# Two fused transformer layers: the next pair's norm moved out of the opening's units, VectorE's first round written out, the first MLP chunk computed by sequence

## The reference

```python
h = (x - mu) * jax.lax.rsqrt(var + LN_EPS)
h = h * (1.0 + scale[:, None, :]) + shift[:, None, :]
q = (h @ Wq.T) ...; c_kv = h @ Wkd.T; k = (c_kv @ Wku.T) ...; v = (c_kv @ Wvu.T) ...
out = softmax(mask(q k / sqrt(d))) @ v;  x = x + out @ Wo.T        # layer 0
...
h = ada_rms(x, time_emb, ln1_w, ln1_tw);  attention as above, 8 heads  # layer 1
x = res + ctx @ Wo.T
h = ada_rms(x, time_emb, ln2_w, ln2_tw)
mlp = jax.nn.silu(h @ Wg.T) * (h @ Wu.T) @ Wd.T
return res + mlp
```

## Time and profile before

| | us |
|---|---|
| median of 3 runs (lowest, highest) | 1760.81 (1760.7, 1761.95) |
| the profiled execution | 1759.8 |
| its span, first to last instruction | 1758.0 |
| PE busy, share of the span | 1703.3, 97% |
| DVE busy | 1148.6, 65% |
| ACT busy | 943.9, 54% |
| POOL busy | 407.1, 23% |

### The profile page before, as it was taken

One profiled execution on the slowest core, in us unless ns is written; L12 is line 12 of the kernel. 1 busy time (PEld: TensorE's weight loads), 2 busy tenths in 40 slices (PEclk: granted clock), 3 DMA queues, 4 the chain that ended last, 5 costly groups with the idle time before them and its releaser, 6 DMA issues.

```text
span 1758.0 us, 37788 instructions
## 1 busy us (share of the span) xinstructions
PE 1703.3 (97%) x12440; PEld 929.4 (53%) x12440; DVE 1148.6 (65%) x2850; ACT 943.9 (54%) x2769; POOL 407.1 (23%) x569
## 2 busy tenths in 40 slices
PE   6777999999999999999999999999999999999999
PEld 3445545555555545565455555555455554556444
DVE  6757675766768568675677767686576866767320
ACT  3936475453855447364674547555484645735320
POOL 3648694111211011011110212110120111102120
PEclk9797999999999999999999999999999999999999
DMA  8966599454866359472793548753584717935310
GB/s 257 166 189 115 159 249 218 92 83 115 194 142 114 76 138 194 96 129 67 175 190 79 91 118 174 163 104 85 123 199 97 139 59 168 198 79 97 115 60 25
DMA packets 527228, 234.24 MB, mean 133 GB/s; under 512 B 476336, under 2 KB 493744, under 8 KB 527024
## 3 DMA queue, kind: packets, MB, share of 16 engines
q1 hardware_dynamic: 511472, 175.09, 49.9%
q10 hardware_dynamic: 15552, 56.63, 10.3%
HBM read 90.09 MB, written 16.78 MB: 61 GB/s over the span
## 4 chain that ended last, share of the span: by engine, by line
PE 82%; DMA 3%; DVE 1%; issue 1%; ACT 0%; SPq 0%; DVEq 0%; ACTq 0%
PE up L1522 9%; PE up L1523 9%; PE up L1524 9%; PE gate L1522 9%; PE gate L1523 9%; PE gate L1524 9%; PE y L1524 4%; PE y L1523 4%; PE y L1522 4%; PE bank L1522 4%; PE bank L1524 4%; PE bank L1523 4%; PE bank L1549 2%; DMA prob_t<-prob 2%; PE bank L1593 2%; PE bank L1557 1%
## 5 line engine op out<-in xcount | busy, mean ns | idle before, releaser
L907 ACT ACTIVATE bank<-bank,low 128x128 f32<-128x128 f32 (+2 forms) x768 | 302.5, 395 | 66.6 <-DVE low L1164 36.9
L731 POOL TENSOR_TENSOR inner_t<-inner,inner_t 128x512 f16<-128x512 f32 x128 | 150.9, 1179 | 637.4 <-ACT inner_t L1103 637.3
L1171 DVE TENSOR_TENSOR prob<-bank,prob 128x512 f16<-128x512 f32 (+1 forms) x304 | 192.7, 634 | 42.9 <-ACT prob L916 41.6
L916 ACT ACTIVATE prob<-bank 128x512 f16<-128x512 f32 (+1 forms) x304 | 169.5, 558 | 59.1 <-DMA prob_t<-prob 41.1
L1477 DVE SCALAR_TENSOR_TENSOR silu<-silu,gate 128x512 f32<-128x512 f32 x128 | 87.9, 687 | 167.7 <-ACT silu L1097 166.6
L1522 PE MATMUL gate<-mlp,ring 128*128 128x512 f16 x512 | 193.9, 379 | 2.1 <-DVE silu L1477 1.2
L1522 PE MATMUL up<-mlp,ring 128*128 128x512 f16 x512 | 193.8, 379 | 0.6 <-DVE inner L1487 0.6
L1524 PE MATMUL gate<-mlp,ring 128*128 128x512 f16 x512 | 194.0, 379 | 0.0
L1523 PE MATMUL gate<-mlp,ring 128*128 128x512 f16 x512 | 193.9, 379 | 0.0
L1524 PE MATMUL up<-mlp,ring 128*128 128x512 f16 x512 | 193.9, 379 | 0.0
L1523 PE MATMUL up<-mlp,ring 128*128 128x512 f16 x512 | 193.9, 379 | 0.0
(11 more groups left out here) (183 smaller groups left out, 4050.5 us busy)
## 6 DMA issues: line engine op xcount, KB each, us to landing
ring<-wgu_dram ACTq DMA_DIRECT2D x108, 512.0 KB, 3.9
x_in<-x_dram SPq DMA_DIRECT2D x18, 512.0 KB, 3.8
x_res<-x_mid SPq DMA_DIRECT2D x16, 512.0 KB, 3.0
wgu_dram<-ring SPq DMA_DIRECT2D x16, 512.0 KB, 3.5
out_dram<-x_res SPq DMA_DIRECT2D x32, 256.0 KB, 2.3
inner_t<-wd_t_dram SPq DMA_DIRECT2D x4, 1024.0 KB, 9.5
ring<-wg_t_dram SPq DMA_DIRECT2D x16, 256.0 KB, 4.2
ring<-wu_t_dram SPq DMA_DIRECT2D x16, 256.0 KB, 4.6
```

Of the source, the lines that this page charges most:

```text
L731: pool.tensor_tensor(inner_t[:, 1, f, :], inner[:], inner_t[:, 0, f, :], ALU.subtract).then_inc(inner_low, 1)
L907: ins = act.activation(bank_[:, at:at + wid], bank_[:, at:at + wid], ACT.Exp, bias=low[:, j % BANKS, k:k + 1], scale=-1.0, accum_out=total)
L916: act.activation(terms(prob_place(n, g)[:, 0, :], layer, j), terms(work_bank[USE[f"unit{layer}", j] % BANKS][:], layer, j), ACT.Copy).then ...
L1171: dve.tensor_tensor(terms(place[:, 1, :], layer, j), terms(work_bank[USE[name] % BANKS][:], layer, j), terms(place[:, 0, :], layer, j), AL ...
```

## The change

Four edits:

- DVE's first round is written out ahead of its loop with the constant pair, so that `FIRST_PARTS` holds on DVE too.
- The first round's `FIRST_PARTS` begin with 4, 0 and not with 0, 4: the four parts of chunk 0 stand ahead of `fill0.0`.
- These four parts become `opening_part`: gate of sequence 0, up of sequence 0, gate of sequence 1, up of sequence 1, each 12 matmuls with 256 columns. Each gate part waits only for the low halves of its own sequence.
- In the opening, the next pair's `ln_stats` go to `out1b`, ahead of each `add`, its `ln_apply` behind `fill4`, and POOL's `ln_root` to `fill4.0`, ahead of `root`.

```diff
-FIRST_PARTS = [0, 4, 3, 1, 2, 1, 0, 0, 2, 1, 4, 0, 2, 2, 4, 0, 0, 4, 3, 1, 2, 3, 1, 2, 1, 1, 2, 1,
+FIRST_PARTS = [4, 0, 3, 1, 2, 1, 0, 0, 2, 1, 4, 0, 2, 2, 4, 0, 0, 4, 3, 1, 2, 3, 1, 2, 1, 1, 2, 1,
...
@@ GpSimd, layers @@
+                    if m is None and step == "fill4.0":
+                        for s in BOTH:
+                            ln_root((n[0], n[1] + 1), s)
                     if step in ("fill2.0", "fill4.0"):
                         for s in BOTH:
                             root(n, ("fill2.0", "fill4.0").index(step), s)
-                    if step in LN_STATS:
+                    if m is not None and step in LN_STATS:
...
@@ VectorE, units @@
-                    if step in LN_STATS:
+                    if m is not None and step in LN_STATS:
                         ln_stats((n[0], n[1] + 1), LN_STATS[step])
-                    elif step in LN_APPLY:
+                    elif m is not None and step in LN_APPLY:
...
@@ VectorE, finish @@
                 for s in BOTH:
+                    if m is None and layer == 1:
+                        ln_stats((n[0], n[1] + 1), s)
                     add(n, layer, s, 1)
...
@@ VectorE, layer1, behind fill4 @@
+                if m is None:
+                    for s in BOTH:
+                        ln_apply((n[0], n[1] + 1), s)
...
@@ VectorE, rounds @@
-            with dve.Fori(0, NP - 1) as i:
-                layer0((i, 1), (i, 0))
-                layer1((i, 1), (i, 0))
+            layer0((None, 1), (None, 0))
+            layer1((None, 1), (None, 0))
+            with dve.Fori(0, NP - 2) as i:
+                layer0((i, 2), (i, 1))
+                layer1((i, 2), (i, 1))
...
@@ TensorE @@
+            def opening_part(part):
+                s, kind = part // 2, part % 2
+                n = (None, 0)
+                bank_, full = ((gbank, g_full), (ubank, u_full))[kind]
+                tokens = slice(s * TOK, (s + 1) * TOK)
+                if kind == 0:
+                    need(pe, low_made, count(n, LOW_USES, LOW_USE["fill4", s, 1] + 1))
+                if s == 0:
+                    if kind == 0:
+                        pe.wait_ge(chunk_split, 1)
+                    need(pe, d_read, count(n, DT, DT - 1 + kind))
+                for c in range(CH):
+                    w = tuple(ring[:, 0, kind, half, c, :] for half in range(2))
+                    ins = product(bank_[:, tokens], w, cut(mlp_t, slice(None), c, tokens),
+                                  c == 0, c == CH - 1)
+                if s == 1:
+                    ins.then_inc(full, 1)
```

More of the change, by code:

```diff
@@ L1738, in layer1 @@
                 between(m, "end")
+            def opening_part(part):
[15 more added lines that the diff above has]
+                    ins.then_inc(full, 1)
             def mlp_part(n, part):
+                if n[0] is None and n[1] == 0 and part < 4:
+                    opening_part(part)
+                    return
                 if part < 4 * FCH:
```

## The result

| | before | after |
|---|---|---|
| median of 20 runs each, in turn on the same chip, us | 1761.84 | 1764.55 |
| lowest and highest, us | 1759.13, 1764.86 | 1759.86, 1768.37 |
| the profiled execution, us | 1759.8 | 1765.89 |
| its span, us | 1758.0 | 1764.1 |

The ratio of the medians is 1.0016, with a 95% interval of 1.0010 to 1.0022: the change is 2.7 us slower. That is less than the 0.2% taken as the bound, but the interval lies wholly above 1, the time lies outside the range, and the sign is the opposite of the forecast's.

What follows compares the result with a forecast made beforehand. PE was taken to bound the steady rounds, so only the opening and first round could give time: -3.6 - 0.2 + 0.5 - 0.1 = -3.4, 1757.4 us for the median; range 1755.0 to 1760.2.

Steps and rivals of the forecast that it cites:

- The units, -3.6: Opening's layer 1 units: without the norm on DVE, ACT's last copy comes 3.6 us earlier; bounds -1.0 and -4.0.
- The norm's new place: Opening's handover: statistics hide in DVE's waits for PE; POOL's root queue makes the first scaling 1.0 us later.
- The second scaling: RMS norm at the last fill: POOL makes its root by 176.75, as before (176.76), so it does not come later.
- Chunk 0 by sequence, and `lat`: Up to the second fill, -0.2 us; then +0.5 for later conversions, with 0.4 of PE's wait ahead of `lat`.
- The rival of the clock: Output projections after the units: if the clock stays low through both, +10.4 us, 1767.8 us; chance 0.04.
- If the clock rose earlier, it would not grow: Opening's units: an earlier clock rise would not raise the 3.6 us gain, since ACT holds the pace.
- The first round, -0.1 with bounds of -1.7 and +1.5: DVE following `FIRST_PARTS`: -1.1 at chunk 4's gate step, +0.4 around unit 20, +0.6 given back.
- The gate step ahead of unit 20: First round: chunk 15's gate step moves ahead of unit 20's low half; PE's scores wait 1.05 us more.
- the 0.6 for what an earlier PE gives back by waiting for others: First round, 223 to 300 us: full DMA engines make an earlier PE wait, returning 0.6 of the 1.1 us gained.
- the first round takes it back: Rival: earlier PE only waits longer at full DMA engines (+0.8), conversions cost 1.5; sum -1.5, 1759.3 us; chance 0.15.
- the sign of error: PE's idle time from 223 to 300 us growing by more than 1 would show the forecast wrong.
- The steady rounds are PE's, every PE instruction there stays, and nothing in this change can shorten them: From 420 us PE is busy throughout, so only the opening and first round can give time.

Runs made afterwards that it cites:

- best1: Changed kernel with POOL's roots reordered, chunk 15's gate step back, 104 unread matmuls in the opening's last eight layer 1 units, 30 VectorE memsets: 1.0005 to before.
- after_gate15: Changed kernel with chunk 15's gate step put back at unit 21, behind unit 20's low half, in VectorE's first round: ratio to before 1.0008.
- after_gates: Changed kernel with the gate steps of chunks 4 and 15 both put back in VectorE's first round: ratio to before 1.0008.

## Why the prediction was wrong

- **The units, -3.6: right.** -3.74, by ACT's pace; of the nine other kernels with the norm's move eight gained 3.5 to 3.8 there, and best1, with unread matmuls in the units, 2.8.
- **The norm's new place: right.** The statistics hid behind the projections, and the roots cost the 1.0 us of POOL's queue at the last fill that was written down. The second scaling, which was to stay in place, came 0.6 us late as well. Swapping the roots gives 1.0 us back at `kv`.
- **Chunk 0 by sequence, and `lat`: nearly right.** The 256-column matmuls lie 0.109 us apart at full clock, and the wait ahead of `lat` is 0.40 as forecast. From the fill to `kv` 0.7 us were to be gained (the 1.0 that the fill was late, 0.2, less 0.5), 0.15 were: the first gate matmul came 3.56 us behind the fill, not 3.3, and chunk 0 took 5.41 us, not 5.2, as the fills and the first three gate matmuls ran at the lower clock.
- **The rival of the clock: the right mechanism, the wrong point and size.** It asked whether the clock would have risen by the projections and gave it 0.04, "PE is the fuller now, not the emptier". The clock rose earlier, which made PE the emptier by time, and in the profiled execution it fell again just ahead of the projections. That cost 1.5 us, not 10.4. "If the clock rose earlier, it would not grow" was the place to ask what an early rise does later.
- **The first round, -0.1 with bounds of -1.7 and +1.5: failed.** It was +3.15. PE's place, followed from `kv` matmul by matmul in both traces, gives the parts: 1.3 us gained at chunk 5's gate, as described; 0.6 lost at the inner step behind it and 1.3 at POOL's splitting by 246 us; 1.8 at the late transfer of 281; 1.3 at unit 20 and 0.9 to the clock behind it; 1.4 won back by 366. The gate step ahead of unit 20 cost the 1.1 us that were forecast. The term that failed is the 0.6 for what an earlier PE gives back by waiting for others: POOL and the one transfer alone took 3.1. The rival "the first round takes it back" had this mechanism, with 0.8 for the whole stretch. The tanh's old time was no guide either, since ACT's copy ahead of it came 2.0 us later, behind a transfer. PE's idle time grew by 3.2 us where more than 1 was named as the sign of error. These waits differ from one execution to the next: the same first round took 197.50 us in the kernel with the roots swapped. Putting the one step back gave 2.9 us in one trace and about 1.4 in the medians (1.0016 to 1.0008).
- **"The steady rounds are PE's, every PE instruction there stays, and nothing in this change can shorten them": the step that failed most.** Nothing shortened them, but they could become longer, and PE's full rows hid that PE is only just ahead of VectorE's low halves in the units. Moving TensorE's loop by 48 instructions costs 3.6 us in five rounds; moved by 256, they are within 0.7 us of before. No term and no rival of the sum allowed for that, and it alone is more than the 2.7 us by which the medians differ.

In the profiled pair the three differences make -1.3 + 3.15 + 3.6 = 5.4 of the 6.1 us; 0.7 is the start's own spread. What stays open: how a load of code slows a transposing transfer, and why the peel in the old order costs 0.08% when its gap is worth so little.

## What to carry to other kernels

Before calling a loop untouched, ask where its code now lies: a few instructions ahead of it can cost more than the edit gains, and a control with as many unread instructions tells the two apart. When a stretch on a slower clock gets shorter, look for where the clock's low time moves to. An in-order step brought forward must be priced by the latest of what it waits for in the new schedule, and by what stands ahead of that input on its own engine, not by that input's old time.

## What the runs showed of the hardware

- **Loop position.** 24 unread matmuls ahead of TensorE's loop (48 instructions) made five rounds 3.6 us longer (1030.64 to 1034.27). With the loop moved by 128 matmuls (256 instructions) they took 1030.95, by 384 (104, 256 and the 24 of chunk 0; 768 instructions) 1031.23. Other distances were not tried. The trace shows code being loaded in the rounds; the transfers of one round, 602 to 809 us after (packets, MB, share):

```profile
q8 instruction: 13, 0.21, 0.4%
q14 instruction: 13, 0.11, 0.1%
```

The Trainium skill, "Runtime: NRT & Kernel Launch", section "Instruction fetch mechanics", says that an engine's code is refilled by DMA in blocks of 16 KiB, 256 instructions, and that the cost is mostly hidden. The 13 packets of 0.21 MB in q8 agree with the block's size (those in q14 are half as large). Its length agrees too: shifts by 256 and 768 instructions leave the loads of q8 where they were in the round and cost nothing, one of 48 moves them and costs. That it is hidden differs: PE shows no wait for code, yet the position cost 0.7 us a round through the transfers.
- **Code loads and transposing transfers.** A transfer of 3.2 us with no load of TensorE's code beside it took 4.6 on average over the seven traces in which one fell beside it. How a load slows it, no run here shows.
- **VectorE's gap.** 0.37 us at one fixed instruction per loop round, gone when the loop moved by 30 instructions.
- **The clock.** Idle time of TensorE can cost twice: as itself, and as 1.2 GHz over the full stretch behind it (the change at 155 to 158 us, the kernel with the norm alone at 176 and 183). With the same instructions the place of the fall differs between executions (155 us in the change; 148 and 150 in after_gate15 and after_gates, with the same opening). Unread matmuls in the idle time kept the clock up at 110 and 175 us.
